# Attention block on one NeuronCore: key products of two column blocks taken in turn with transposes of the probabilities

## The reference

```
x = x + xattn(layernorm(x), ctx, ctx, ...)
q = split_heads(Q @ Wq + bq); k = split_heads(K @ Wk + bk); v = split_heads(V @ Wv + bv)
scores = einsum('bhqd,bhkd->bhqk', q, k) / sqrt(HEAD_DIM)
attn = softmax(scores, axis=-1)
out = einsum('bhqk,bhkd->bhqd', attn, v) @ Wo + bo
x = x + attn_ref(layernorm(x), ...)      # 16 heads over the 128 tokens, normalized
x = x + ffn_ref(x, ...)                  # argmax over four experts, gelu, normalized
```

## Time and profile before

| what | value |
|---|---|
| median of three runs | 516.69 us (516.57 to 518.53) |
| profiled execution | 517.64 us |
| its span | 515.9 us |
| granted TensorE clock, mean | 0.995 |
| TensorE busy | 498.3 us |
| VectorE, ScalarE, POOL busy | 299.4, 259.8, 42.2 us |

### The profile page before, as it was taken

The page is one execution under the profiler, slowest core; times in us unless marked ns, Lnnn a source line. Parts: engine busy times, 40 slices in busy tenths (PEclk is TensorE's granted clock), DMA queues, the critical chain, the costliest instruction groups (busy, mean ns, idle before and its releaser), DMA issues.

```text
span 515.9 us, 9281 instructions
## 1 busy us (share of the span) xinstructions
PE 498.3 (97%) x3762; PEld 383.1 (74%) x3762; DVE 299.4 (58%) x583; ACT 259.8 (50%) x396; POOL 42.2 (8%) x34
## 2 busy tenths in 40 slices
PE   8999999999999999999999999999999999999995
PEld 6886776777777777887877778757695777877664
DVE  4647523546455542436286474588479988965532
ACT  4130119494858641238267649476255735754310
POOL 0220000000298000000000000000002010000000
PEclk9999999999999999999999999999999989999999
DMA  8800000000440022220300000495586998874000
GB/s 290 344 0 1 1 1 0 3 0 3 151 168 11 1 83 83 81 83 1 142 3 2 0 3 1 147 422 249 180 327 248 361 402 302 334 292 164 1 20 20
DMA packets 11497, 63.52 MB, mean 123 GB/s; under 512 B 1600, under 2 KB 2112, under 8 KB 4544
## 3 DMA queue, kind: packets, MB, share of 16 engines
q1 hardware_dynamic: 11168, 62.67, 32.1%
q10 hardware_dynamic: 288, 0.27, 0.2%
HBM read 62.41 MB, written 0.52 MB: 122 GB/s over the span
## 4 chain that ended last, share of the span: by engine, by line
PE 79%; ACT 9%; DVE 7%; issue 4%; POOL 1%; POOLq 0%; ACTq 0%; DVEq 0%
PE ps L1147 35%; PE ps L1217 11%; PE ps L1231 6%; PE ps L1201 5%; ACT Pm L447 4%; PE ps L1460 3%; PE ps L1462 3%; PE ps L1461 3%; PE ps L1478 3%; PE ps L1604 2%; PE ps L1409 1%; ACT PT L455 1%; PE ps L1141 1%; PE ps L1243 1%; DVE w1L L979 1%
## 5 line engine op out<-in xcount | busy, mean ns | idle before, releaser
L455 ACT COPY PT<-ps 128x512 f32<-128x512 f32 x128 | 68.5, 592 | 28.9 <-PE ps L1217 28.9
L745 DVE TENSOR_SCALAR_CACHE_REDUCE Pm<-ps,small 128x512 f32<-128x512 f32 x96 | 66.4, 748 | 28.5 <-PE ps L1201 28.4
L1217 PE MATMUL ps<-ident,Pm 128*128 128x128 f32 x512 | 69.3, 277 | 2.9 <-ACT Pm L447 2.9
L1217 PEld LDWEIGHTS ps<-ident,Pm 128*128 128x128 f32 x512 | 56.5, 141 | 17.7 <-issue 11.0
L447 ACT ACTIVATE Pm<-Pm,small 128x2048 f32<-128x2048 f32 x32 | 64.3, 2011 | 7.4 <-DVE Pm L745 7.3
L725 DVE SCALAR_TENSOR_TENSOR KrL<-ps,small,KrH 128x512 fp32r<-128x512 f32 x32 | 23.9, 747 | 59.2 <-ACT KrH L433 59.2
L1147 PE MATMUL ps<-ctxH,wkH 128*128 128x512 f32 x124 | 51.3, 414 | 0.0
L1147 PE MATMUL ps<-wvH,ctxH 128*128 128x512 f32 x124 | 50.1, 404 | 1.0 <-DVE V L734 1.0
L1147 PE MATMUL ps<-ctxL,wkH 128*128 128x512 f32 x124 | 48.6, 392 | 0.0
L1147 PE MATMUL ps<-ctxH,wkL 128*128 128x512 f32 x124 | 48.5, 391 | 0.0
L1147 PE MATMUL ps<-wvH,ctxL 128*128 128x512 f32 x124 | 48.4, 390 | 0.0
(11 more groups left out here) (219 smaller groups left out, 859.8 us busy)
## 6 DMA issues: line engine op xcount, KB each, us to landing
w1raw<-in_W SPq DMA_DIRECT2D x16, 1024.0 KB, 6.1
w2raw<-in_W SPq DMA_DIRECT2D x16, 1024.0 KB, 5.5
raw<-in_ctxT SPq DMA_DIRECT2D x7, 1024.0 KB, 5.0
woF<-in_ffn_Wo SPq DMA_DIRECT2D x4, 1024.0 KB, 9.2
wo<-in_wo SPq DMA_DIRECT2D x2, 1024.0 KB, 4.8
ctx_first<-in_ctxT SPq DMA_DIRECT2D x4, 256.0 KB, 5.0
wv_raw<-in_xWv SPq DMA_DIRECT2D x2, 512.0 KB, 7.4
wq<-in_xWq SPq DMA_DIRECT2D x1, 1024.0 KB, 12.2
```

The costliest lines, as they stand in the source:

```text
L455: act.copy(PT[:, c % 2, i, :, :].rearrange("p k t -> p (k t)"), ps[:, t_bank(p, c, i), :]).then_inc(pt_done, 1)
L745: dve.tensor_scalar(Pm[:, i, c * CH:(c + 1) * CH], ps[:, i, :], -1.0, mx[:, p % 2, i, c - 1:c] if c else NOT_YET, ALU.mult, ALU.min, accum ...
L1217: last = pe.transpose(ps[:, t_bank(p, c, i), j * P:(j + 1) * P], Pm[:, i, c * CH + j * P:c * CH + (j + 1) * P], ident[:])
```

## The change

Only TensorE's program is changed. The waits at the head of `keys` and of `probs_T` become functions of their own, `keys_ready` and `probs_ready`, and a single transpose becomes `prob_T`. A new function, `keys_among_probs_T(p, c, c_probs, i0)`, issues the 12 products of a key block with one transpose behind each of the first eight: the four of head i0, then the four of head i0 + 1, of block c_probs of pass p - 1. For c = 0 it takes the keys of block 2 and the transposes of heads 0 and 1; the keys were a block behind these transposes. For c = 1 it takes the keys of block 3 and the transposes of heads 2 and 3; the keys were a block behind the scores that follow these transposes. The products, the transposes and the banks are the same, and the last turn, which has no keys, is as before.

```diff
-            def keys(p, c):
+            def keys_ready(p, c):
...
                 if p and c == 1:
                     pe.wait_ge(s_done, p * C * HPG)
+
+            def keys(p, c):
+
+                keys_ready(p, c)
+                g = p % G
+                f = slice(g * P, (g + 1) * P)
                 product(ps[:, K2_BANK if p and c == 1 else K_BANK, :], [(w[:, k, f], t[:, k, :]) for k in range(KT)
...
+            def prob_T(p, c, i, j):
+
+                return pe.transpose(ps[:, t_bank(p, c, i), j * P:(j + 1) * P],
+                                    Pm[:, i, c * CH + j * P:c * CH + (j + 1) * P], ident[:])
...
+            def keys_among_probs_T(p, c, c_probs, i0):
+
+                keys_ready(p, c)
+                f = slice(p % G * P, (p % G + 1) * P)
+                for k in range(KT):
+                    for part in range(3):
+                        n = 3 * k + part
+                        w, t = ((wkH, ctxH[c]), (wkL, ctxH[c]), (wkH, ctxL[c]))[part]
+                        last = pe.matmul(ps[:, K_BANK, :], w[:, k, f], t[:, k, :], start=(n == 0), stop=(n == 3 * KT - 1))
+                        if n < 2 * JT:
+                            i, j = i0 + n // JT, n % JT
+                            if j == 0:
+                                probs_ready(p - 1, c_probs, i)
+                            turned = prob_T(p - 1, c_probs, i, j)
+                            if j == JT - 1:
+                                turned.then_inc(t_mm, 1)
+                last.then_inc(k_mm, 1)
...
                 for c in range(C):
-                    probs_T(p - 1, c, 0)
-                    probs_T(p - 1, c, 1)
+                    if c == 0 and more:
+                        keys_among_probs_T(p, 2, c, 0)
+                    else:
+                        probs_T(p - 1, c, 0)
+                        probs_T(p - 1, c, 1)
                     if p == G + 3 and c == 2:
                         masks(0)
-                    if c == 0 and more:
-                        keys(p, 2)
                     if c == 0 and p == NP:
                         first_experts(1)
                     if c:
                         weighted_values(p - 1, c - 1)
-                    probs_T(p - 1, c, 2)
-                    probs_T(p - 1, c, 3)
+                    if c == 1 and more:
+                        keys_among_probs_T(p, 3, c, 2)
+                    else:
+                        probs_T(p - 1, c, 2)
+                        probs_T(p - 1, c, 3)
                     if more:
                         scores(p, c)
-                        if c == 1:
-                            keys(p, 3)
```

More of the change, by code:

```diff
@@ L1160, in keys @@
                     pe.wait_ge(wk_rest_split, 1)
-                f = slice(g * P, (g + 1) * P)
                 if p and c == 1:
                     pe.wait_ge(s_done, p * C * HPG)
+            def keys(p, c):
+                keys_ready(p, c)
+                g = p % G
+                f = slice(g * P, (g + 1) * P)
                 product(ps[:, K2_BANK if p and c == 1 else K_BANK, :], [(w[:, k, f], t[:, k, :]) for k in range(KT)
@@ L1204, in scores, with probs_ready @@
                             last.then_inc(s_mm, 1)
-            def probs_T(p, c, i):
+            def probs_ready(p, c, i):
                 pe.wait_ge(exp_done, HPG * p + i + 1)
@@ L1215, in probs_T @@
                     pe.wait_ge(pt_done, HPG * n + i - 1)
+            def prob_T(p, c, i, j):
+                return pe.transpose(ps[:, t_bank(p, c, i), j * P:(j + 1) * P],
+                                    Pm[:, i, c * CH + j * P:c * CH + (j + 1) * P], ident[:])
+            def probs_T(p, c, i):
+                probs_ready(p, c, i)
                 for j in range(JT):
-                    last = pe.transpose(ps[:, t_bank(p, c, i), j * P:(j + 1) * P],
-                                        Pm[:, i, c * CH + j * P:c * CH + (j + 1) * P], ident[:])
+                    last = prob_T(p, c, i, j)
                 last.then_inc(t_mm, 1)
+            def keys_among_probs_T(p, c, c_probs, i0):
[14 more added lines that the diff above has]
+                last.then_inc(k_mm, 1)
             def weighted_values(p, c):
```

## The result

The changed kernel took 531.37 us (median of four runs, 530.42 to 532.41) beside 517.56 us for the kernel before (516.57 to 518.53): a ratio of 1.0255, with a 95% interval of 1.0227 to 1.0284, 13.8 us slower. The profiled execution took 532.01 us.

A forecast was written before the change was run, and what follows sets the result against it. TensorE, 97% busy, was taken as the bound, except one point of each pass where ScalarE ends last. Part one's 6.6 plus part two's 4.2 made 10.8 us; from 517.64 profiled, less 0.95 for the median: 527.5 us, range 521.5 to 531.5.

The forecast's parts named there:

- passes two to four: Head 1's late copy delays ScalarE's exponential of head 3, so TensorE waits longer: 1.05 us a pass, 3.15 in all.
- pass six, to S0: From pass five's last scores to pass six's first, the late copy delays head 3's exponential and the scores: 1.60 us.
- pass seven, to S0: From pass six's last scores to pass seven's first, other work in the exponential's place, same result: 1.6 us more.
- plain second blocks and pass five's: Block 3's keys among block 1's transposes: 0.06 us a pass in passes one to four and six, a seventh part for five; 0.35.
- shuffles, pass five: ScalarE's eight shuffles follow the late copy of head 3, delaying later copies and the transposes needing them: 1.6 us.
- masks, pass seven: Mask transposes wait for VectorE's low half of block 3's keys, behind later scores and evacuations: 1.9 us.
- statistics, pass six: VectorE's statistics, formerly in a gap, now stand ahead of the next evacuations: between 0 and 0.7, taken as 0.3 us.
- free: Rival: transposes wholly hidden under key products, pair 0.23 us, sum -1.0, time 515.7 us; chance 0.05.
- cheap: Rival: pair 0.26 to 0.32 us on TensorE, sum 2.0 to 7.9, time 518.7 to 524.6 us; chance 0.11.
- dear rival: Each key's weight load is exposed behind a transpose, pair 0.45 us, sum 20.6, time 537.3 us; chance 0.07.
- The bound at the changed point: ScalarE, up to head 3's exponential, ends last at this point of each pass; rival that it doesn't: 521.7 us, chance 0.05.
- The exponential's wait: Sign: TensorE's transposes wait for ScalarE's exponentials some 8 us in place of 2.9, about 1.4 in passes two to four.

The follow-up runs named there:

- part one alone: Against the changed kernel: only block 2's keys among block 0's transposes, block 3's keys back behind the scores; 525.01 us against 517.74 for the kernel before.
- exponential ahead: Changed kernel with ScalarE's exponential of head 3 put ahead of its copy of head 1 of block 0; 526.70 us against 517.74 for the kernel before.
- part two alone: Against the changed kernel: only block 3's keys among block 1's transposes, block 2's keys as before the change; 524.32 us against 517.74 for the kernel before.
- all three: Changed kernel with head 3's exponential before head 1's copy, pass seven's low key half before evacuations, pass five's shuffles behind block 3; 520.22 us against 517.44 before.
- pairs behind the scores: Against the changed kernel: block 3's keys behind the scores, among block 2's transposes of heads 0 and 1; block 2's keys in a block; 521.17 us against 517.74 before.
- two behind a key: Only block 2's keys mixed with block 0's transposes, two transposes behind each of the first four keys; 518.74 us against 517.39 for the kernel before.
- ScalarE relieved: Kernel before the change, with the high half of block 1's keys made by VectorE instead of ScalarE from pass one on; 515.78 us against 517.44.
- low keys ahead: Changed kernel with VectorE's low half of block 3's keys ahead of block 1's score evacuation, pass seven only; 526.01 us against 517.44 for the kernel before.
- shuffles later: Changed kernel with ScalarE's eight shuffles of pass five behind the copies of block 3 instead of block 1; 530.34 us against 517.44 for the kernel before.

## Why the prediction was right, and where it was short

Term by term, in us. "Measured" is the changed kernel; where one term hides in another's stretch, the experiment that separates it is named.

| term | predicted | measured |
|---|---|---|
| pass one | 0.16 | 0.09 |
| passes two to four | 3.15 | 2.98 |
| pass six, to S0 | 1.60 | 1.56 |
| pass seven, to S0 | 1.60 | 1.60 (part one alone) |
| pairs of pass five, part one | 0.1 | 0.05 |
| plain second blocks and pass five's | 0.35 | 0.23 without pass five's, which is in the next line |
| shuffles, pass five | 1.6 | 1.67 |
| masks, pass seven | 1.9 | 3.29, of it 1.85 at full clock (exponential ahead) |
| statistics, pass six | 0.3 | 0.39 (part two alone) |
| sum | 10.8 | 11.9 |

- *The pair.* 0.35 was taken and 0.344 measured. With 0.345 for it the free, the cheap and the dear rival fall: the border of the earlier trace rows did show the price, by the second key product and not by the first, which is again recorded 0.03 us behind the transpose and 0.48 long. The Trainium skill, "TensorE: Matmul & The Clock Gate", section "Back-to-back issue gap", would give for such a pair, as an estimate from its figures, 81 + 131 = 212 ns; the measured 344 doesn't agree, and by the page the change would have been a gain.
- *The bound at the changed point.* ScalarE, shown from both sides: the loss goes when its order is mended, and the kernel before gains when it is relieved.
- *The exponential's wait.* "Some 8 us in place of 2.9": 8.4, with 1.30 in each of passes two to four for the 1.4 forecast. The list counts seven waits: the six passes of the forecast, and one of 0.56 us in the last turn that stands in the kernel before too.
- *The shuffles, the masks' wait and the statistics* came where they were put, with 1.5 us for the first and 2.6 for the second, as forecast.
- *The step that failed* is the size of the masks' term. The wait was right and its price was not: the work behind it was costed by rows at full clock, and it ran at half for 3.4 us, 1.44 more.
- *Outside the turns.* The sum had nothing there, and the profiled execution has 1.6 behind the last scores and 0.9 ahead of the first. The 1.6 is clock again (below). The 0.9 lies in the first 28 products of the identity with itself, the same instructions in both kernels, recorded over 6.18 us in place of 5.22. In all nine experiments the time ahead of the first scores is 0.6 to 1.3 us above the profiled execution of before, in the last one too, which has none of the change. It does not always lie at that place: in the last one and in part two alone those 28 products take 5.17 and 5.22. So the change is not needed for it, and why the profiled execution of before began soonest isn't shown.
- *TensorE's busy time* "should hardly move" and moved by 5.6 us. Part one alone, with all its waits and no low clock but at the end, has 498.2. So the longer records at low clock are part of the 5.6; how much is theirs, and how much that of records inside pairs, was not separated.

By the medians, the change cost 3.0 us more than the sum of 10.8. Of that, 1.1 lies in the turns, where the 1.44 of the clock stands against 0.3 less elsewhere, and about 1.6 behind them; these two are read from one profiled execution each and so need not sum to 3.0. The other 0.9 of the 3.9 us is the time from which the forecast started: the median of the kernel before was 516.69 us of three runs, and is 517.56 with a fourth.

That the result fell inside the range is in part luck. Two of its four runs, 532.01 and 532.41, lie above the top of 531.5, and the median lies above the 525 to 530.5 that the forecast kept for itself. That range was made for the price of the pair, which came out as taken; the low clock that used most of it up had no term in it.

## What to carry to other kernels

Mixing two blocks of products on one engine delivers the first block later, at the pace of the mix; before doing it, follow the last product of the first block to its reader, and that reader's next instruction in order, since an engine that works in order passes the delay on to what stands behind. The price of the mix itself is read from a border between the two kinds that the trace already has, from the second product behind it. And where a change makes the busiest engine wait for some microseconds, set aside a term for its clock behind the wait, and where a wait is taken away look for the work of other engines that it covered.

## What the runs showed of the hardware

TensorE's granted clock fell to 0.5, its 1.2 GHz level, for stretches of about 3.4 or 6.8 us that differ from kernel to kernel, and this carries most of what the sum missed. Windows late in the execution, one of the changed kernel, two of the kernel before, and one of part one alone (columns as above):

```profile
434.00:441.00 7.00, 7.00 (x23) 5.73 (x23) 4.40 (x9) 3.79 (x3) 0.00 (x0) 0.51 1.01 428
```

```profile
420.00:423.00 3.00, 2.90 (x22) 2.13 (x21) 2.38 (x6) 2.72 (x3) 0.00 (x0) 0.80 1.01 429
423.00:426.00 3.00, 3.00 (x10) 2.38 (x9) 2.96 (x4) 1.95 (x2) 0.00 (x0) 0.63 1.01 429
```

```profile
415.00:445.00 30.00, 29.01 (x127) 20.85 (x126) 26.70 (x33) 18.20 (x19) 1.47 (x2) 1.00 0.97 383
```

At a clock of either 1.00 or 0.50, the first is all but some 0.1 us at the low level, and the two of the kernel before hold (3.00 x 0.20 + 3.00 x 0.37) / 0.50 = 3.4 us of it. The same program runs there in all kernels. In all eleven profiled executions TensorE had waited 0.87 to 0.89 us for VectorE's attnT; the low level began some 2 us behind the end of that wait in seven of them, and not in the other four. What follows the last scores goes with it:

| low clock in that stretch | kernels | end against before |
|---|---|---|
| none | part one; pairs behind the scores; two behind a key; ScalarE relieved | -1.4 to -1.7 |
| 3.4 us | before; part two; exponential ahead; all three | -0.2 to +0.3 |
| 6.8 us | the change; low keys ahead; shuffles later | +1.6 to +1.7 |

So each 3.4 us at the low level costs about 1.6 us at the end, and 1.44 behind the masks. Executions of one kernel differ in it too: the four runs of part one alone took 522.92 and 523.23 us at a mean granted clock of 0.999 and 0.998, and 526.79 and 526.84 at 0.993 and 0.990. The four of the changed kernel all had 0.990 to 0.992, where the 17 runs of before that stood beside the last experiments had 0.993 to 0.999: each run of the changed kernel had more of the low level than any of those.

What decides it stays open. The wait of 2.6 us at the masks was followed by the low level in three profiled executions (the change, part two alone, the shuffles later) and by the full one in the kernel with the exponential ahead, one of whose other runs took 527.37 us at 0.990. Where the wait was taken away the low level was not seen at the masks. The waits of 1.3 us for the exponentials and of 1.5 us behind the shuffles were followed by the full level in every profiled execution. So the long wait goes with the low level, but doesn't by itself force it.
